# Pairwise-interaction kernel: 62 units of products folded instead of 44, 28 of them by accumulating DMAs

## The reference

```python
e = jnp.stack([tbl_0[ids[:, 0]], ..., tbl_39[ids[:, 39]]], axis=1)   # 512 x 40 x 64
vi = x[:, i_idx, :]
vj = x[:, j_idx, :]
viW = jnp.einsum('bpd,pde->bpe', vi, W)
out = jnp.einsum('bpe,bpe->bp', viW, vj)
...
h = jnp.concatenate([z, dense_ctx], axis=1)
h = jnp.maximum(h @ W_top1 + b_top1, 0.0)     # 796 -> 512
h = jnp.maximum(h @ W_top2 + b_top2, 0.0)     # 512 -> 256
y = h @ W_top3                                # 256 -> 1
```

## Time and profile before

| | |
|---|---|
| median of 3 runs | 353.68 us (353.11 to 353.86) |
| the profiled execution, own time | 353.03 us |
| its span in the profile | 351.1 us |
| PE busy | 344.3 us (98%) |
| DVE busy | 256.7 us (73%) |
| Pool busy | 227.4 us (65%) |
| granted TensorE clock | 1.00 over the whole span |

### The profile page before, as it was taken

One profiled execution on the slowest core, in us unless ns is written; L12 is line 12 of the kernel. 1 busy time (PEld: TensorE's weight loads), 2 busy tenths in 40 slices (PEclk: granted clock), 3 DMA queues, 4 the chain that ended last, 5 costly groups with the idle time before them and its releaser, 6 DMA issues.

```text
span 351.1 us, 4306 instructions
## 1 busy us (share of the span) xinstructions
PE 344.3 (98%) x1682; PEld 115.1 (33%) x1682; DVE 256.7 (73%) x246; ACT 70.3 (20%) x112; POOL 227.4 (65%) x176
## 2 busy tenths in 40 slices
PE   7999999999999999999999999999999999999997
PEld 3222333233332333333333333333233333334342
DVE  3965877786878787789889987898998989970010
ACT  1243703333213030303040302103021030000011
POOL 5665466566466466368895879888889999970000
DMA  7646231221212221822112220212110000000000
GB/s 213 231 148 199 79 111 49 82 80 23 80 31 71 80 78 39 329 84 71 56 32 69 75 75 16 69 66 78 60 67 10 0 2 0 0 2 0 0 0 0
DMA packets 10740, 24.18 MB, mean 69 GB/s; under 512 B 3537, under 2 KB 4305, under 8 KB 10594
## 3 DMA queue, kind: packets, MB, share of 16 engines
q1 hardware_dynamic: 6482, 19.72, 16.0%
q0 software_dynamic: 4096, 4.20, 4.9%
q10 hardware_dynamic: 144, 0.00, 0.0%
HBM read 23.91 MB, written 0.00 MB: 68 GB/s over the span
## 4 chain that ended last, share of the span: by engine, by line
PE 97%; ACT 1%; DVE 1%; issue 0%
PE u L440 52%; PE zp L461 20%; PE xp L415 8%; PE u L471 7%; PE xp L402 3%; PE u L428 2%; PE u L507 2%; PE u L479 2%; ACT xq L373 1%; ACT xt L368 1%; DVE prod L552 0%; PE xp L512 0%; PE xp L514 0%; DVE prod L554 0%; DVE prod L541 0%
## 5 line engine op out<-in xcount | busy, mean ns | idle before, releaser
L552 DVE TENSOR_TENSOR prod<-u,xq 128x1024 f32<-128x1024 f32 x180 | 206.8, 1214 | 44.4 <-PE u L440 39.9
L440 PE MATMUL u<-xt,w_ring 64*128 64x512 f32 x760 | 189.9, 619 | 1.6 <-ACT xt L368 1.3
L331 POOL DMA_INDIRECT gath<-in_tbl,ids_sb x128 | 124.2, 970 | 75.8 <-DMA gath<-in_tbl,ids_sb 42.3
L339 POOL TENSOR_TENSOR prod<-prod 128x1024 f32<-128x1024 f32 x44 | 102.9, 2367 | 10.0 <-DVE prod L552 9.7
L440 PEld LDWEIGHTS u<-xt,w_ring 64*128 64x128 f32 x760 | 63.9, 185 | 117.9 <-DVE prod L552 63.4
L461 PE MATMUL zp<-prod,sel_sb 128*32 128x512 f32 x604 | 72.5, 597 | 0.0
L368 ACT ACTIVATE xt<-xp 128x512 f32<-128x512 f32 x20 | 12.0, 598 | 197.8 <-PE xp L402 153.9
L373 ACT ACTIVATE xq<-xt 32x512 f32<-32x512 f32 x80 | 50.2, 627 | 2.1
L461 PEld LDWEIGHTS zp<-prod,sel_sb 128*32 128x32 f32 x604 | 17.5, 109 | 51.1 <-issue 46.3
L530 DVE TENSOR_SCALAR xq<-late,row_sb 128x1024 f32<-128x1024 int32 x32 | 22.0, 746 | 11.6 <-PE xp L415 6.9
L415 PE MATMUL xp<-xq,late 128*64 128x512 f32 x128 | 28.3, 595 | 0.7 <-ACT xt L368 0.7
(11 more groups left out here) (22 smaller groups left out, 39.0 us busy)
## 6 DMA issues: line engine op xcount, KB each, us to landing
w_ring<-in_w_cell SPq DMA_DIRECT2D x24, 512.0 KB
late<-in_ids_small SPq DMA_DIRECT2D x4, 512.0 KB, 5.2
gath<-in_tbl,ids_sb POOLq DMA_INDIRECT x128
late<-in_w_top SPq DMA_DIRECT2D x1, 1792.0 KB
late<-in_small SPq DMA_DIRECT2D x3, 512.0 KB
late<-in_small SPq DMA_DIRECT2D x2, 256.0 KB
late<-in_w_top SPq DMA_DIRECT2D x1, 512.0 KB
wd_sb<-in_w_diag SPq DMA_DIRECT2D x1, 320.0 KB
```

The costliest lines, as they stand in the source:

```text
L331: pool.indirect_dma_start(gath[:, g % GR, t, half, :], None, tables[f], bass.IndirectOffsetOnAxis(ap=ids_sb[:, t, f:f + 1], axis=0),).then ...
L339: pool.tensor_tensor(prod[:, lo % PR, :, :], prod[:, lo % PR, :, :], prod[:, hi % PR, :, :], ALU.add).then_inc(folded, 1)
L440: mm = pe.matmul(u[:, n % UR, a, :], w_ring[rows, q % RW, at * P:(at + 1) * P], xt[rows, moving % XR, :], start=True, stop=True)
L552: dve.tensor_tensor(prod[:, n % PR, :, :], u[:, n % UR, :, :], x, ALU.mult).then_inc(prod_ready, 1)
```

## The change

`FOLDED` and `FOLDS_AFTER` get new entries. 31 batches, that is 62 units, are folded, in place of 22 batches (44 units, as the count of the profile's row for the fold shows too). By m the folded batches were 3, 4, 6 and 9 for m = 6, 7, 8 and 9. Now they are 1, 2, 3, 3, 5, 8 and 9 for m = 3 to 9. The 28 units of blocks 6 to 15 are no longer added by an instruction of Pool: Pool begins a DMA that reads the HI slot and accumulates it into the LO slot, both on the chip. Each DMA has one of 8 semaphores in turn. The 34 units of blocks 16 to 19 are added by Pool as before. PE waits before a folded batch for both of its units.

```diff
-FOLDED = {6: 3, 7: 4, 8: 6, 9: 9}
-
-FOLDS_AFTER = [0] * 22 + [2, 2, 2, 2, 2, 3, 1, 3, 7, 0]
+FOLDED = {3: 1, 4: 2, 5: 3, 6: 3, 7: 5, 8: 8, 9: 9}
+
+DMA_BELOW = 8
+
+FOLDS_AFTER = [0] * 10 + [1, 1, 0, 2, 1, 1, 2, 0, 2, 2, 1, 1, 1, 1, 2, 0, 3, 1, 3, 3, 13, 0]
...
+DMA_FOLDS = [u for u in FOLDS if u[0] < 2 * DMA_BELOW]
+POOL_FOLDS = [u for u in FOLDS if u[0] >= 2 * DMA_BELOW]
...
+FR = 8
...
             def fold(k, q):
                 lo, hi = AT["unit", k, q, LO], AT["unit", k, q, HI]
+                if (k, q) in DMA_FOLDS:
+                    i = DMA_FOLDS.index((k, q))
+                    if i >= FR:
+
+                        pool.wait_ge(dma_folded[i % FR], 16 * (i // FR))
+                    pool.wait_ge(prod_ready, PRODS[hi + 1])
+                    pool.dma_start(prod[:, lo % PR, :, :], prod[:, hi % PR, :, :],
+                                   accum_op=ALU.add).then_inc(dma_folded[i % FR], 16)
+                    return
                 pool.wait_ge(prod_ready, PRODS[hi + 1])
                 pool.tensor_tensor(prod[:, lo % PR, :, :], prod[:, lo % PR, :, :], prod[:, hi % PR, :, :],
-                                   ALU.add).then_inc(folded, 1)
+                                   ALU.add).then_inc(pool_folded, 1)
...
                 pe.wait_ge(prod_ready, PRODS[batch_last(b) + 1])
-                if is_folded:
-                    pe.wait_ge(folded, FOLDS.index(units[-1]) + 1)
+                for unit in units if is_folded else []:
+                    if unit in DMA_FOLDS:
+                        i = DMA_FOLDS.index(unit)
+                        pe.wait_ge(dma_folded[i % FR], 16 * (i // FR + 1))
+                    else:
+                        pe.wait_ge(pool_folded, POOL_FOLDS.index(unit) + 1)
```

More of the change, by code:

```diff
@@ L256, in program @@
         prod_ready = sem("prod_ready")
-        folded = sem("folded")
+        pool_folded = sem("pool_folded")
+        dma_folded = [sem(f"dma_folded{r}") for r in range(FR)]
         summed = sem("summed")
```

## The result

| | before | changed |
|---|---|---|
| median | 353.73 us (353.11 to 353.86, 4 runs) | 365.03 us (361.72 to 366.36, 4 runs) |
| profiled execution, own time / span | 353.03 / 351.1 us | 364.46 / 362.6 us |

The ratio is 1.031 with a 95% interval of [1.0279, 1.0341]: the change made the kernel slower by 11.3 us. The forecast was 3.2 us faster, and the time lies outside the range.

What follows compares the result with a forecast made beforehand. DVE's work plus DVE's gaps bound the part with slots. Saved gaps of -5.6 us and a +2.4 us wait at slot 79 gave -3.2: 353.03 to 349.8, plus 0.65 for the median, 350.5 us; range 348.0 to 364.

Steps and rivals of the forecast that it cites:

- What bounds the kernel, and the saving of 5.6 us: Slots: DVE's work plus its gaps set the time; fewer sum rounds shorten the gaps by 3.0 and 2.6 us.
- The issue on Pool (1.25 us): Pool's queue: each of 28 DMA issues takes 1.25 us (bounds 0.4 to 2.5), mostly within Pool's pauses.
- The third rival: Pool's queue: issues from about 1.7 us each make batches late, +3 to +8, about 358 us; chance 0.08.
- The DMA work of a fold (2.6 us): DMA engines: a fold reads 512 KB twice and writes it once, taken as 2.6 us.
- one read after the other: DMA engines: a fold's two reads follow one another, 1.05 MB, 2.3 us at best or 2.9 at 367 GB/s.
- All of these have 1 to 2 us to spare, with one exception: Folded batches' sums: every fold lands in time with 1 to 2 us left, except at the dense layers' loads.
- at most 1.68 us: Pool's gathers: from the end of the issue to the landing a gather takes at most 1.68 us.
- The second rival: `sum_batch` after close accumulates: folds miss their cover from about 2.9 us; at 3.2, +10, 364 us; chance 0.25.
- The term of 2.4 us at slot 79: Sum at slot 79: block 11's folds land late beside the dense layers' loads; +2.4 us (0 to 6).
- the fourth rival: Merged groups hide more or a bank's hand-over shows: half the gain, about 352.9 us; chance 0.07.

Runs made afterwards that it cites:

- experiment 2: Changed kernel with its 28 accumulating DMAs made plain copies of the HI slot over the LO slot: 349.68 us, ratio 0.9905.
- experiment 3: Changed kernel with the dense layers' loads behind the last piece of W (W1_AT 23, not 12): 358.23 us, ratio 1.0128.
- the first: Changed kernel with its 28 accumulating DMAs and PE's waits on them left out: 347.64 us, ratio 0.9844.
- eleventh: The 348.65 us kernel (moved folds, late loads, FOLD_LAG 12) with the dense layers' loads back behind piece 12 of W: ratio 1.0044, about 355 us (median 358.2).
- the fifth: Changed kernel with FOLD_LAG 12 in place of 10, so folded batches are summed two slots later: 359.02 us, ratio 1.0149.
- tenth: The 348.65 us kernel (folds moved on Pool's queue, late dense layers' loads, FOLD_LAG 12) with FOLD_LAG back at 10: 351.13 us, ratio 0.9934.
- the seventh: Changed kernel with FOLD_LAG 12, late dense layers' loads, and folds moved on Pool's queue, mostly one behind each field's gathers: 348.65 us, ratio 0.9831.
- the sixth: Changed kernel with FOLD_LAG 12 and the dense layers' loads behind the last piece of W, Pool's queue order kept: 355.87 us, ratio 1.0058.

## Why the prediction was wrong

The direction was wrong. By its steps:

- **What bounds the kernel, and the saving of 5.6 us:** right. The run without folds saved 5.6 us, and the gaps behind merged groups came out at 4.76 and 3.32 for 4.8 and 3.3. Of the saving nothing was lost in the changed kernel; it was covered by waits.
- **The issue on Pool (1.25 us):** 1.0 us measured, inside the bounds. The third rival falls.
- **The DMA work of a fold (2.6 us):** right for a lone fold. The windows over the first one, which is alone but for gathers, and then over the first copy of experiment 2 (columns as in the earlier trace rows):

```profile
81.00:82.00 1.00, 1.00 (x12) 0.13 (x4) 0.00 (x0) 0.00 (x0) 0.81 (x1) 1.00 0.67 131
82.00:83.00 1.00, 1.00 (x8) 0.30 (x4) 0.00 (x0) 0.00 (x0) 0.70 (x2) 1.00 1.02 197
83.00:84.00 1.00, 1.00 (x8) 0.72 (x8) 0.81 (x1) 0.23 (x1) 0.69 (x2) 1.00 1.08 197
84.00:85.00 1.00, 1.00 (x6) 0.20 (x4) 0.58 (x2) 0.97 (x2) 0.78 (x1) 1.00 0.27 66
...
81.00:82.00 1.00, 1.00 (x10) 0.25 (x4) 0.00 (x0) 0.00 (x0) 0.00 (x0) 1.00 0.76 311
82.00:83.00 1.00, 1.00 (x6) 0.24 (x5) 0.08 (x1) 0.00 (x0) 0.83 (x1) 1.00 0.53 217
```

  The four shares add up to 3.0 us; the gathers alone make about 0.12 in each of these windows (0.12 from 85 to 86 us), which leaves 2.6. The mean of all 28 is 2.8 to 2.9. The bound "one read after the other" fits, and a copy's 1.3 to 1.5 us is half of it. By the Trainium skill ("Collectives: The Full Stack", the fold count and the bandwidth ceiling), which puts a reducing copy at half the rate because of its two reads: the runs agree, 2.8 to 2.9 us for an accumulate and 1.3 to 1.5 for a copy.
- **The step that failed: "All of these have 1 to 2 us to spare, with one exception".** It let a lone fold land 4.2 us behind its issue and a pair 6.8, as if the folds had the DMA engines to themselves, and it followed Pool's queue as if a gather still landed in 1.68 us. The four waits outside slot 79, forecast at nothing, cost DVE 1.8, 0.9, 1.0 and 2.5 us over the gaps of the run without folds (1.70, 1.70, 1.73, 0.75); another gap gave 0.5. Together 6.8 us. The chain of work that ended last goes through an accumulate at four of these five places (start of its issue, time to its landing; below them SP's row of a piece of W):

```profile
100.34 10.14 DMA prod<-prod
182.10 6.12 DMA prod<-prod
211.26 7.25 DMA prod<-prod
231.04 11.69 DMA prod<-prod
...
100.15 0.33 SPq L289 DMA_DIRECT2D w_ring<-in_w_cell  x1
```

  With the issue counted, the forecast's numbers are 5.5 us (1.25 + 4.2) for a lone fold and 8.1 (1.25 + 6.8) for the second of a pair. The first line is the second of a pair, the next two are begun by themselves and the last is the third of three; the first of these three, begun at 229.87 us, ended PE's wait of 2.26 us at 237.73, the dearest of the four. The lengths are over all 28 folds in experiment 3 and all 28 copies in experiment 2:

```profile
DMA to landing us min/median/max: 4.7/6.8/12.0
DMA to landing us min/median/max: 2.9/3.4/10.1
```

  So an undisturbed fold was quicker than forecast, and the median one was not. At slot 49 Pool was in time: the pair's issue ended 7.3 us before its sum, near the forecast's 7.5, and the landing took 8.8 from there. SP began a piece of W at 100.15, 182.99, 206.60 and 229.12 us, shortly before or beside each of these, and the prediction had no piece of W in any landing but slot 79's. Late gathers come on top at the last one: the gathers before these three folds held Pool 4.78 us in place of 1.68. That the pieces of W are what made the first three late is read from the trace; no run moves them. The gathers' "at most 1.68 us" was too short even in the kernel before:

```profile
96.16 0.94 POOL L331 DMA_INDIRECT gath<-in_tbl,ids_sb  x1 [2.39 <-DMA gath<-in_tbl,ids_sb]
```

  The second rival had waits in four other batches and gathers pushed back behind folds, but put its threshold at 2.9 us a fold, its effect at +10 from 3.2. It took hold with folds of 2.6 to 2.9 us.
- **The term of 2.4 us at slot 79:** right in place and mechanism, mis-sized by a factor of four. It measured 13.20 - 3.32 = 9.9 us. Pool was 4.8 us later than I had it, because its gathers had waited 3.60 and 3.84 us; the pair then took 12.7 us from its last issue (147.8) to the sum (160.5) where I had 10.1; and some 2.4 us are the lower clock of TensorE in the sums behind the wait (5.47 - 3.63 and 1.59 - 1.06), a cost that no step of mine had.

Two slips change nothing: the five multiplies read as "in the loads' window" ran from 136.3 to 142.0 us, mostly ahead of it (DVE's multiplies took 206.5 us against 206.8 all the same), and the fourth rival's own terms, -2.8 + 2.4, give 353.3 us and not 352.9.

The sum as it would have been right: -5.6 + 9.9 + 6.8 = +11.1 us, against 11.4 between the two profiled executions. Its parts are backed by runs: the saving by the first, the time of an accumulate on the DMA engines by the second, the collision by the third and eleventh, the missing cover by the fifth and tenth, the places on the queue by the seventh against the sixth. How much of a fold's or a gather's delay is order in the queue and how much is sharing the engines, with pieces of W above all, wasn't separated.

## What to carry to other kernels

Work that is moved onto a DMA queue isn't free because the engine that begins it is idle: put its transfer time into the queue ahead of everything that stands behind it, add every load of another queue that falls beside it, and follow the queue again with those times before calling a deadline met. An accumulating DMA within the chip cost twice a copy here. Where a stall hits TensorE, allow for what the next matmuls lose if the clock falls; and where a transfer must land in time, a big load that has no deadline of its own belongs elsewhere: three small edits (places, cover, the load's place) turned a ratio of 1.031 into one of 0.983.

## What the runs showed of the hardware

- An accumulate of 512 KB within on-chip memory took 2.6 us of the 16 DMA engines alone and 2.8 to 2.9 in the mean, a copy 1.3 to 1.5 us; Pool's issue took 1.0 us for the one and 0.59 us for the other.
- From the start of its issue to its landing an accumulate took 4.7 us at least, 6.8 in the median and 12.0 at most (experiment 3); a copy 2.9, 3.4 and 10.1 (experiment 2).
- Pool waited 3.60 to 8.14 us for gathers of 32 KB begun behind pairs of accumulates, beside loads of another queue, where 1.68 was usual; behind one accumulate alone they landed as before.
- TensorE's granted clock fell to 0.5 at 154 us, after PE had stood still for 1.93 us, and was whole again some 4 us after the sums had resumed at 160.54; the 30 records behind the longer wait took 5.47 us and not 3.63. In experiment 3 a wait of 2.66 us left it at 1.00.
